# Picking one tile of source rows in 16 with TensorE instead of gathering it, in the message sums of a graph network

## The chip, the cores and the metric

The kernel runs as one program on one core of one Trainium2 chip. The metric is the device time of one execution in microseconds (us), lower is better. The same program is timed in several executions; the median is what counts.

## The reference, cut to what matters

A graph of 3125 nodes and 100,000 edges, sorted by target node, goes through four layers. The change lies in the fourth, of which this is the part that matters:

```python
src_f = x[src_idx]
dst_f = x[dst_idx]
msg_in = jnp.concatenate([src_f, dst_f, ew], axis=-1)
h = jax.nn.silu(msg_in @ mW1 + mb1)
messages = (h @ mW2 + mb2) * ew
aggregated = jax.ops.segment_sum(messages, dst_idx, num_segments=num_nodes)
```

The kernel multiplies each node by the source part and by the target part of `mW1` once, ahead of the edges. For each edge it then needs the 128 numbers of its source node (the gathered row), the 128 numbers of its target node, their sum through silu, times the edge weight, added up by target node. The product with `mW2` follows after the sums.

## The kernel before, in words

Edges are cut into 800 tiles of 125, four tiles are a quad (200 quads), and nodes into 25 windows of 125. Since edges are sorted by target, each quad touches one window, or two at a border: a step is one quad with one window, and there are 224 steps (`TEAMS`). Steps are grouped by four (`AHEAD`), which below is called a round: 56 rounds.

`message_sums` gives each engine its own loop. They meet only by semaphores; each engine works its own list strictly in the order written.

- GpSimd (POOL), `gather_quads`, line 553: for each quad four indirect DMAs, one per tile, each fetching 125 rows of `node_table` from HBM into a ring of 20 quads (`rows`). It waits for `kept`, which says that the ring's place is free.
- SyncE (SP), `pass_quads`: for each quad it frees the place of the quad four before, once DVE has used it (`added`), then waits for the quad's rows (line 572) and tells DVE with `here`. It also loads the indices (`now`).
- ScalarE (ACT), in step k: `copy_turned(k+1)` (line 1008), `widen(k+2)` (line 1003), the load of a one-hot tile (line 998), and silu in `apply(k)` (line 1013).
- TensorE (PE), in step k: `spread_rows(k)` (line 1051, target rows into `zp`), `turn_rows(k+2)` (line 1043, transposes the one-hot of target nodes), `sum_team(k-1)` (line 1060, sums messages by target node).
- VectorE (DVE), in step k: `weigh(k-1)` (lines 1092 and 1093), then z = `zp` + gathered rows (line 1110), `weigh_rows(k+2)` (line 1086), `add_team(k-2)` (line 1100).

Two waits matter for what follows. z of step k needs the gathered rows and `spread_rows(k)`. And `turn_rows(k+2)` needs `weigh_rows(k+2)`, which DVE issues only behind z of step k: so within a step PE's list goes on only after z.

Of the kernel before, what the change touches and what calls it, by code (L numbers as in the profile page):

```python
# [45 lines left out]
BIG = 1.0e30  # L46
ROUND = 12582912.0
EPS = 1e-5
GROUPS = (WIN + 3) // 4
CHUNK = 261  # L50
SIDE = 2 * CHUNK
# [357 lines left out]
def landed(i, dmas=1):  # L409

    return 16 * dmas * (i + 1)
# [121 lines left out]
def begin(eng, *sems):  # L533

    for sem in sems:
        eng.sem_inc(sem, AHEAD)
# [4 lines left out]
    return k - lag + 1 + AHEAD  # L541


def gather_quads(pool, table, rows, now, held_up, staged, kept, rows_in):
# [12 lines left out]
def pass_quads(sp, g, now, staged, rows_in, here, kept, step_done, held):  # L557

    def stage(n, group):
        sp.dma_start(now[:, n, :], g.tile_src[:, bass.ds(HALF * HALF * group, HALF * HALF)]).then_inc(staged[n], 16)  # L560

    def free(quad):
        last = sp.value_load(g.quad_done[0:1, bass.ds(quad, 1)], min_val=1 + AHEAD, max_val=TEAMS + AHEAD)
        sp.wait_ge(step_done, last)
        sp.sem_inc(kept, 1)

    def quads(i):
        for q in range(RING):
            if q >= held or not isinstance(i, int):
                free(RING * i + q - held)  # L570
            sp.wait_ge(rows_in[q], landed(i, HALF))
            sp.sem_inc(here, 1)  # L572
            if q % HALF == HALF - 1:
                stage(q // HALF, STAGES * i + STAGES + q // HALF)

    sp.sem_inc(kept, RING)
    for n in range(STAGES):
        stage(n, n)
    quads(0)
    with sp.Fori(1, QUADS // RING) as i:  # L580
        quads(i)
    for n in range(STAGES):
        sp.wait_ge(staged[n], landed(QUADS // RING))
# [372 lines left out]
                add_team(TEAMS - 2 + q, q + 2, ws[q])  # L956


def message_sums(nc, g, table, own):

# [3 lines left out]
    with Scope(nc) as sc:  # L964
# [8 lines left out]
        turn = sc.ps("turn", [P + 1, 2, 512])  # L973
        zp = sc.ps("zp", [P, 2, HALF, D])
        sums = sc.ps("sums", [P, 2, 512])
        kept, here = sc.sem("kept"), sc.sem("here")
        names = ("held_up", "acc_clear", "made", "weighed", "turned", "copied", "spread", "added", "active", "tailed", "weighted", "summed", "accd")
        held_up, acc_clear, made, weighed, turned, copied, spread, added, active, tailed, weighted, summed, accd = (sc.sem(x) for x in names)
# [4 lines left out]

        @block.gpsimd
        def _(pool):
            gather_quads(pool, table, rows, now, held_up, staged, kept, rows_in)

        @block.sync
        def _(sp):
            pass_quads(sp, g, now, staged, rows_in, here, kept, added, HALF)  # L990

        @block.scalar
        def _(act):
            begin(act, made, copied, active)

            def load_hot(k, q):
                act.wait_ge(made, after(k, AHEAD))
                act.dma_start(hot[:, q, :], g.hots[bass.ds(k, 1), :, :].rearrange("a p n -> (a p) n")).then_inc(hot_in[q], 16)

            def widen(k, m, q):  # L1000
                act.wait_ge(hot_in[q], landed(m))
                act.wait_ge(summed, after(k, AHEAD))
                act.copy(onehot[:, q, :, 0:P], hot[:, q, :].rearrange("p (j n) -> p j n", n=P)).then_inc(made, 1)

            def copy_turned(k, p):
                act.wait_ge(turned, after(k))
                act.wait_ge(spread, after(k, 2))
                act.activation(onehot_t[:, p, :], turn[:, p, 0:HALF * P], ACT.Identity).then_inc(copied, 1)

            def apply(k, p):  # L1010
                act.wait_ge(added, after(k))
                act.wait_ge(weighted, after(k, 2))
                act.activation(hidden[:, p, :, :], z[:, p, :, :], ACT.Silu).then_inc(active, 1)

            for q in range(AHEAD):
                load_hot(q, q)
            for q in range(2):
                widen(q, 0, q)
            copy_turned(0, 0)
            rounds = TEAMS // AHEAD  # L1020
            with act.Fori(0, rounds - 1) as i:
                for q in range(AHEAD):
                    k = AHEAD * i + q
                    copy_turned(k + 1, 1 - q % 2)
                    widen(k + 2, i + (q + 2) // AHEAD, (q + 2) % AHEAD)
                    load_hot(k + AHEAD, q)
                    apply(k, q % 2)
            for q in range(AHEAD):
                k = TEAMS - AHEAD + q
                copy_turned(k + 1, 1 - q % 2)  # L1030
                widen(k + 2, rounds - 1, (q + 2) % AHEAD)
                apply(k, q % 2)

        @block.tensor
        def _(pe):
            begin(pe, turned, spread, summed)

            def turn_rows(k, q):
                pe.wait_ge(made, after(k))
# [23 lines left out]
            def team(k, q):  # L1063
                spread_rows(k, q % 2)
                turn_rows(k + 2, (q + 2) % AHEAD)
                if not (isinstance(k, int) and k == 0):
                    sum_team(k - 1, (q - 1) % AHEAD)

            turn_rows(0, 0)
            turn_rows(1, 1)  # L1070
            for q in range(AHEAD):
                team(q, q)
            with pe.Fori(1, TEAMS // AHEAD) as i:
# [5 lines left out]
        def _(dve):  # L1079
            begin(dve, weighed, added, tailed, weighted, accd)  # L1080
            dve.memset(g.acc[:, :, :], 0.0).then_inc(acc_clear, 1)
            dve.wait_ge(acc_clear, 1)

            def weigh_rows(k, q):
                dve.wait_ge(summed, after(k, AHEAD))
# [26 lines left out]
                if not (first and k < 2):  # L1112
                    add_team(k - 2, p)

            def teams(i):
# [5 lines left out]
            weigh_rows(1, 1)  # L1121
            teams(0)
            with dve.Fori(1, TEAMS // AHEAD) as i:
                teams(i)
            weigh(TEAMS - 1, 1)
            add_team(TEAMS - 2, 0)
            add_team(TEAMS - 1, 1)
# [580 lines left out]
def prepare(nc, g, sc, src, dst, edge_weight, x, nodes):  # L1708
# [21 lines left out]
    g.step_quad, g.step_slot, g.quad_done = steps[32:33, 0:TEAMS + 1], steps[64:65, 0:TEAMS + 1], steps[96:97, 0:QUADS]  # L1730
    g.place = sc.sb("place", [1, 3 * (TEAMS + 1)], I32)
    g.pair = sc.sb("pair", [1, 2 * TEAMS], I32)
    g.tile_src = nc.dram_tensor("tile_src", (P, TILES + RING * HALF), I32, kind="Internal").ap()

    with Scope(nc) as s1:
# [32 lines left out]
        slot = s1.sb("slot_", [P, TEAMS])  # L1768
        over = s1.sb("over", [P, QUADS])
        slot_rows = s1.sb("slot_rows", [SIXTY, FIFTEEN, P], F16)  # L1770

        with Scope(nc) as s2:
            names = ("dst_in", "pre_in", "src_in", "ew_in", "pre_set", "zeroed", "drawn", "step", "bordered", "totalled", "compared", "summed")
            dst_in, pre_in, src_in, ew_in, pre_set, zeroed, drawn, step, bordered, totalled, compared, summed = (s2.sem(k) for k in names)
            names = ("sourced", "src_cut", "dst_parted", "src_parted", "ew_cut", "ew_left", "natural", "tiled", "picks", "picked", "kept", "x_in", "slotted", "rows_turned", "rows_kept", "tabled")
            sourced, src_cut, dst_parted, src_parted, ew_cut, ew_left, natural, tiled, picks, picked, kept, x_in, slotted, rows_turned, rows_kept, tabled = (s2.sem(k) for k in names)
# [8 lines left out]
            def _(sp):  # L1785
# [3 lines left out]
                sp.dma_start(src_i[:, :], src.rearrange("(r l) -> r l", l=rlen)).then_inc(src_in, 16)  # L1789
                sp.dma_start(ew_row[:, :], edge_weight.rearrange("(r l) -> r l", l=rlen)).then_inc(ew_in, 16)  # L1790
                wide(sp, x[:, :, :], by_window(nodes), x_in)
                sp.wait_ge(tiled, 1)
                sp.dma_start(g.tile_src, tile_src[:, :]).then_inc(kept, 16)
                sp.wait_ge(kept, 16)
                sp.wait_ge(x_in, 16 * len(PIECES))

            @block.gpsimd
# [29 lines left out]
            def _(dve):  # L1827
# [21 lines left out]
                dve.wait_ge(src_in, 16)  # L1849
                link(dve.tensor_copy(src_row[:, :], src_i[:, :]))  # L1850
                dve.sem_inc(sourced, 1)
                link(dve.tensor_copy(dst_parts[0][:, :], dst_row[:, :]))
                link(dve.tensor_tensor(dst_parts[1][:, :], dst_row[:, :], dst_parts[0][:, :], ALU.subtract))
                dve.sem_inc(dst_parted, 1)
# [528 lines left out]
def layer3(nc, g, a, x, table, out):  # L2383

    with Scope(nc) as sc:
# [22 lines left out]
        message_sums(nc, g, table, pb)  # L2408
# [150 lines left out]
```

## Time and profile before

| | us |
|---|---|
| median of 3 executions | 6612.52 (6611.82 to 6618.84) |
| the profiled execution | 6634.63 |
| its span, first to last instruction | 6632.9 |
| message sums within the span | about 5328 to 6571 |
| mean granted TensorE clock, whole span | 0.786 of full speed |

Over the span PE is busy 64%, DVE 52%, ACT 23%, POOL 60%. These shares are means over stages with different limits; the message sums are one stage, and rows of that stretch of time say what bounds it. A TensorE matmul in fp32 shows as two records here: a line of code that issues four matmuls leaves eight of them. A granted clock of 1.00 is 2.4 GHz, 0.50 is 1.2 GHz; values between are stretches in which it changed.

### The profile page before, as it was taken

The numbers are of one execution on the slowest core, as the hardware profiler recorded it, in microseconds if no ns is written. First come the engines' busy times: TensorE is split into PE (matmuls) and PEld (weight loads), VectorE is DVE, ScalarE is ACT, GpSimd is POOL, SyncE is SP. The second block draws the span as 40 slices with busy tenths as digits, with TensorE's granted clock in tenths as the row PEclk, the third lists the DMA queues.
The fourth block names the chain that finished last, engine by engine and source line by source line (L and its number), as shares of the span: only waits on it lengthen the run. The fifth ranks groups of instructions, "written<-read, shape, count | busy, mean of one in ns | idle before, by whom it ended". The sixth has DMA issues, their size and how long they took to land. (4 is left out here: it accounts for less than half of the span.)

```text
span 6632.9 us, 118789 instructions
## 1 busy us (share of the span) xinstructions
PE 4258.2 (64%) x28231; PEld 3627.6 (55%) x28232; DVE 3436.1 (52%) x8797; ACT 1545.7 (23%) x3206; POOL 3989.5 (60%) x3272
## 2 busy tenths in 40 slices
PE   7868774666666646666666466666664466666665
PEld 6755333555556535556665356665553355555554
DVE  8987225554545564545555645555556533333334
ACT  4764100111111111111111101111111134444443
POOL 0000003888888728878888288888881068888884
PEclk8999986788877777878777677777876777777777
DMA  5863441333333313333333133333331222222221
GB/s 158 216 166 112 119 119 47 87 91 86 90 87 92 91 47 84 87 88 92 92 91 89 46 79 92 92 89 90 89 89 33 52 67 65 66 65 65 66 65 46
DMA packets 599808, 578.37 MB, mean 87 GB/s; under 512 B 244747, under 2 KB 537024, under 8 KB 599702
## 3 DMA queue, kind: packets, MB, share of 16 engines
q0 software_dynamic: 260480, 241.33, 15.7%
q10 hardware_dynamic: 205535, 197.01, 10.2%
q1 hardware_dynamic: 133687, 138.75, 7.8%
q8 instruction: 51, 0.84, 0.1%
q14 instruction: 55, 0.45, 0.0%
HBM read 488.64 MB, written 84.64 MB: 86 GB/s over the span
## 5 line engine op out<-in xcount | busy, mean ns | idle before, releaser
L553 POOL DMA_INDIRECT rows<-row_table,now x2400 | 2967.7, 1237 | 1607.9 <-issue 1566.1
L553 POOL DMA_INDIRECT rows<-node_table,now x800 | 988.5, 1236 | 567.1 <-issue 567.1
L754 PE MATMUL zp<-rows,ident 125*125 x2700 | 975.4, 494 | 543.9 <-SPq L572 543.0
L840 DVE SCALAR_TENSOR_TENSOR z<-zp,own 125x512 f32<-125x512 f32 x672 | 464.8, 692 | 1374.8 <-PE zp L754 1347.9
L765 PEld LDWEIGHTS sums<-values,hot 125*125 125x125 f32 x5376 | 880.3, 225 | 165.5 <-issue 83.4
L751 PE MATMUL zp<-parts,hot_t 125*125 x8100 | 730.4, 249 | 372.0 <-DVE logit L847 264.6
L765 PE MATMUL sums<-values,hot 125*125 125x137 f32 x5376 | 906.9, 321 | 58.7 <-ACT hot L700 34.3
L754 PEld LDWEIGHTS zp<-rows,ident 125*125 125x125 f32 x2700 | 568.2, 234 | 657.9 <-issue 576.6
L751 PEld LDWEIGHTS zp<-parts,hot_t 125*125 125x125 bf16 x8100 | 691.8, 160 | 425.6 <-issue 420.6
L700 ACT CAST hot<-hot 125x500 f32<-125x500 bf16 x672 | 408.6, 608 | 2106.0 <-PE sums L765 1714.7
L851 DVE TENSOR_TENSOR values<-rows,xl 125x512 f32 (+1 forms) x672 | 461.6, 687 | 102.5 <-PE sums L765 80.5
L1043 PE MATMUL turn<-ident,onehot 125*126 125x125 f32 x904 | 179.2, 333 | 472.2 <-issue 451.8
L1110 DVE TENSOR_TENSOR z<-zp,rows 125x512 f32<-125x512 f32 x224 | 154.9, 691 | 630.0 <-SPq L572 495.1
L844 DVE TENSOR_REDUCE bent<-z 125x16 f32<-125x512 f32 x672 | 456.0, 679 | 1.6
L1043 PEld LDWEIGHTS turn<-ident,onehot 125*126 125x126 f32 x904 | 118.3, 169 | 517.7 <-issue 494.7
L1060 PE MATMUL sums<-values,onehot 125*125 125x129 f32 x1792 | 334.6, 349 | 0.0
L1051 PE MATMUL zp<-pb,onehot_t 126*125 x1792 | 332.3, 346 | 2.5
L1335 DVE TENSOR_SCALAR hot<-nodes,src_lo,src_unit 125x522 bf16<-125x522 f16 x896 | 315.1, 416 | 18.1 <-PE bank L1374 17.0
L1051 PEld LDWEIGHTS zp<-pb,onehot_t 126*125 126x125 f32 x1792 | 311.7, 260 | 10.2 <-issue 8.6
L1374 PE MATMUL bank<-hot,hot_dst 125*125 125x261 bf16 x1792 | 268.9, 296 | 67.8 <-DVE hot L1335 37.2
L1060 PEld LDWEIGHTS sums<-values,onehot 125*125 125x125 f32 x1792 | 310.0, 258 | 0.0
L1302 POOL DMA_DIRECT2D spread_slots<-slot_table x56 | 30.3, 541 | 397.7 <-DVE hot_t L1328 344.2
(447 smaller groups left out, 4918.8 us busy)
## 6 DMA issues: line engine op xcount, KB each, us to landing
hot<-hots ACTq DMA_DIRECT2D x896, 122.1 KB
hot_t<-hots_t ACTq DMA_DIRECT2D x678, 122.1 KB
rows<-row_table,now POOLq DMA_INDIRECT x2400, 3.5
counts<-pairs SPq DMA_DIRECT2D x55, 685.1 KB
spread_slots<-slot_table POOLq DMA_DIRECT2D x56, 488.3 KB
hots_t<-hot_t SPq DMA_DIRECT2D x112, 218.8 KB
hots<-hot_dst SPq DMA_DIRECT2D x112, 218.8 KB
pairs<-cells SPq DMA_DIRECT2D x25, 685.1 KB
```

The source lines that it names most:

```text
L553: pool.indirect_dma_start(rows[:, q, j, :], None, table, bass.IndirectOffsetOnAxis(ap=now[:, n, lane + j:lane + j + 1], axis=0)).then_inc( ...
L700: act.copy(hot32[:, q % 2, :], hot[:, q, :]).then_inc(made, 1)
L751: pe.matmul(zp[:, p, j, 0:ROW], hot_t[:, q, j * P:(j + 1) * P], own[part], start=part == 0 and j % 2 == 0, stop=False, skip_group_check=True)
L754: ins = pe.matmul(zp[:, p, 2 * half:2 * half + 2, 0:ROW], g.ident[0:P, 0:P], rows[:, bass.ds(at, 1), 2 * half:2 * half + 2, :].rearrange(" ...
L765: ins = pe.matmul(sums[:, p, 0:ACCW], hot32[:, p, j * P:(j + 1) * P], values[:, p, j, :], start=j == 0, stop=j == HALF - 1)
L840: dve.scalar_tensor_tensor(out=z[:, p, :, :], in0=zp[:, p, :, 0:D], scalar=0.0, in1=rows_of(own_att, HALF), op0=ALU.max, op1=ALU.mult).the ...
L844: dve.tensor_reduce(bent[:, p, :, :], z[:, p, :, :].rearrange("p j (h c) -> p j h c", h=HEADS), AX_X, ALU.add).then_inc(reduced, 1)
L851: dve.tensor_tensor(values[:, q % 2, :, 0:D].rearrange("p j (h c) -> p j h c", h=HEADS), rows[:, bass.ds(at, 1), :, 0:D].rearrange("p a j ...
L1043: ins = pe.transpose(turn[:, q % 2, j * P:(j + 1) * P], onehot[:, q, j, :], g.ident[0:P, 0:P])
L1051: ins = pe.matmul(zp[:, p, j, :], onehot_t[:, p, j * P:(j + 1) * P], own[:, bass.ds(w, 1), :].rearrange("p w f -> p (w f)"), start=True, s ...
L1060: ins = pe.matmul(sums[:, q % 2, 0:width], onehot[:, q, j, 0:P], values[:, q % 2, j, :], start=j == 0, stop=j == HALF - 1)
L1335: dve.tensor_scalar(hot[:, p % AHEAD, j, :], nodes[:, :], g.src_lo[:, s], g.src_unit[:, s], ALU.is_equal, ALU.mult).then_inc(hot_made, 1)
```

## The change

In every fourth quad (q % 4 == 3) the last tile is no longer gathered: 50 tiles of 800 (`PICKS`). Its rows are made on the chip. `pa`, the table's 25 windows of 125 nodes, is still in SBUF. ACT loads the tile's 125 source numbers (halved range, fp16) broadcast over the partitions and copies them into a PSUM bank (`lay`). DVE compares them with the node numbers of all 25 windows, in three cuts of 9, 8 and 8 windows (`point`), which gives one-hots in `at`, free at this time. PE multiplies the 25 one-hots by the 25 windows of `pa` and adds up in the bank `mix` (`pick`, 25 fp32 matmuls in the same three cuts). ACT copies the result to SBUF and stores it to HBM (`store_picked`), and SP loads it into the ring (`fetch`), two quads ahead of its use.

Picks 0 and 1 are made before the first step, pick i+2 in round i, for 48 of the 56 rounds; the last 8 rounds have none. The source numbers are written to HBM in `prepare` (one more DVE instruction on 100x125 and two small DMAs).

```diff
+def by_engine(q, picks):
+    return picks and q % PICK == PICK - 1
...
-            for j in range(HALF):
+            for j in range(HALF - 1 if by_engine(q, picks) else HALF):
                 pool.indirect_dma_start(rows[:, q, j, :], None, table,
...
+            if fetch is not None and q % PICK == PICK - 3:
+                fetch(i, q + 2)
+            if by_engine(q, fetch is not None):
+                hold(sp, rows_in[q], landed(i, HALF - 1), fetching)
+                sp.wait_ge(fetched[q // PICK], landed(i, len(PIECES)))
...
+            def lay(t):
+                act.wait_ge(src_in, landed(t))
+                act.copy(wide_src[:, 0:P], src[:, :]).then_inc(laid, 1)
+                act.wait_ge(laid, t + 1)
+
+            def store_picked(t):
+                act.wait_ge(mixed, len(CUTS) * (t + 2))
+                if not (isinstance(t, int) and t == 0):
+                    act.wait_ge(stored, landed(t - 1, len(PIECES)))
+                act.copy(picked[:, :], mix[:, 0:D]).then_inc(evicted, 1)
+                act.wait_ge(evicted, t + 1)
+                wide(act, store[bass.ds(t, 1), :, :].rearrange("a p f -> (a p) f"), picked[:, :], stored)
...
+            with act.Fori(0, PICKS - 2) as i:
+                four_steps(i)
+                store_picked(i + 2)
+                lay(i + 3)
+                load_src(i + 4)
+            with act.Fori(PICKS - 2, rounds - 1) as i:
+                four_steps(i)
...
+            def pick(t, r):
+                pe.wait_ge(noded, len(CUTS) * t + r + 1)
+                if r == 0 and not (isinstance(t, int) and t == 0):
+                    pe.wait_ge(evicted, t)
+                for w in range(*CUTS[r]):
+                    ins = pe.matmul(mix[:, 0:D], hot_n[:, w, :], pa[:, w, :], start=w == 0, stop=w == WIN - 1)
+                ins.then_inc(mixed, 1)
...
+            def team(k, q, t=None):
                 spread_rows(k, q % 2)
                 turn_rows(k + 2, (q + 2) % AHEAD)
+                if t is not None and q:
+                    pick(t, q - 1)
...
+            def point(t, r):
+                lo, hi = CUTS[r]
+                if r == 0:
+                    dve.wait_ge(laid, t + 1)
+                dve.wait_ge(mixed, len(CUTS) * t + r + 1)
+                dve.tensor_tensor(hot_n[:, lo:hi, :], rows_of(wide_src[:, 0:P], hi - lo), each(nodes[:, lo:hi], P), ALU.is_equal).then_inc(noded, 1)
...
+            def teams(i, picking=True):
                 quads, slots = step_quads(nc, dve, g, AHEAD * i)
                 for q in range(AHEAD):
+                    if picking and q < len(CUTS):
+                        point(i + 2, q)
                     team(i, q, quads[q], slots[q])
```

On TensorE, one step (the second of a round) in the loop over rounds, before:

```order
L436 ISA
L436 TENSOR_LOAD steps
L436 ISA x2
L1048 REGISTER_ALU
L1051 ISA
L1051 MATMUL zp<-pb,onehot_t 125x128 x4
L1039 REGISTER_ALU
L1043 MATMUL turn<-ident,onehot 126x125 x4
L1060 MATMUL sums<-values,onehot 125x129 x4
```

The same step in the changed kernel:

```order
L441 ISA
L441 TENSOR_LOAD steps
L441 ISA x2
L1124 REGISTER_ALU
L1127 ISA
L1127 MATMUL zp<-pb,onehot_t 125x128 x4
L1115 REGISTER_ALU
L1119 MATMUL turn<-ident,onehot 126x125 x4
L1107 ISA
L1111 MATMUL mix<-pa,at 125x128 x9
L1136 MATMUL sums<-values,onehot 125x129 x4
```

Nine matmuls now stand between the transposes and the sums (eight in the third and in the fourth step, none in the first).

On ScalarE, the end of a round in the first loop of the changed kernel, behind the last silu (before, that silu was followed by the loop's branch):

```order
L1044 ACTIVATE hidden<-z 125x512
L1057 ISA
L1059 REGISTER_ALU
L1060 COPY picked<-mix 125x128
L1061 REGISTER_ALU
L143 ISA
L143 DMA picked_nodes<-picked 112x128
L143 ISA
L143 DMA picked_nodes<-picked 13x128
L1052 REGISTER_ALU
L1053 CAST wide_src<-src 125x125
L1049 ISA
```

The copy of the picked rows, two stores and the copy of the next tile's sources into PSUM now stand between two rounds on this engine.

## Rows read from the trace of the kernel before

**Rows 1.** Groups of instructions, 5328 to 6575: shapes, count | busy, mean ns | idle before.
```profile
L553 POOL DMA_INDIRECT rows<-node_table,now x800 | 988.5, 1236 | 567.1 <-issue 567.1
...
L1110 DVE TENSOR_TENSOR z<-zp,rows 125x512 f32<-125x512 f32 x224 | 154.9, 691 | 630.0 <-SPq L572 495.1 <-PE zp L1051 134.2 <-issue 0.2
...
L1100 DVE TENSOR_TENSOR acc<-acc,sums 125x129 f32 x224 | 65.0, 290 | 77.1 <-issue 73.6 <-PE sums L1060 3.0
```

**Rows 2.** Waits, 5328 to 6575: who waited <- for whom: total us, times, longest.
```profile
DVE z L1110 <- SPq L572: 495.1, 142, 6.9
...
DVE z L1110 <- PE zp L1051: 134.2, 75, 3.4
```

**Rows 3.** Timeline, start of the stage: start, us, engine, line.
```profile
5330.92 1.21 POOL L553 DMA_INDIRECT rows<-node_table,now  x1 [323.52 <-issue]
5331.42 0.61 ACT L1003 CAST onehot<-hot 125x500 f32<-125x500 bf16 x1 [23.28 <-DMA hot<-hots]
...
5334.23 2.05 PE L1051 MATMUL zp<-pb,onehot_t 126*125 x8
...
5339.29 0.69 DVE L1110 TENSOR_TENSOR z<-zp,rows 125x512 f32<-125x512 f32 x1 [6.95 <-SPq L572]
```

**Rows 4.** Timeline, end of the stage.
```profile
6561.76 1.21 POOL L553 DMA_INDIRECT rows<-node_table,now  x1 [0.30 <-issue]
...
6565.52 0.69 DVE L1110 TENSOR_TENSOR z<-zp,rows 125x512 f32<-125x512 f32 x1 [3.86 <-SPq L572]
```

**Rows 5.** Timeline, steps that catch up at the full clock, 5930 to 5938.
```profile
5930.36 0.69 DVE L1110 TENSOR_TENSOR z<-zp,rows 125x512 f32<-125x512 f32 x1 [2.47 <-PE zp L1051]
...
5931.23 0.62 PE L1043 MATMUL turn<-ident,onehot 125*126 125x125 f32 x4 [1.02 <-issue]
...
5931.68 1.05 PE L1060 MATMUL sums<-values,onehot 125*125 125x129 f32 x8
...
5934.20 0.69 DVE L1110 TENSOR_TENSOR z<-zp,rows 125x512 f32<-125x512 f32 x1 [0.22 <-PE zp L1051]
...
5937.76 0.69 DVE L1110 TENSOR_TENSOR z<-zp,rows 125x512 f32<-125x512 f32 x1 [0.52 <-PE zp L1051]
```

**Rows 6.** Timeline of DVE, a third and fourth step of a round at the full clock.
```profile
6378.01 0.69 DVE L1110 TENSOR_TENSOR z<-zp,rows 125x512 f32<-125x512 f32 x1 [1.19 <-PE zp L1051]
...
6381.40 0.69 DVE L1110 TENSOR_TENSOR z<-zp,rows 125x512 f32<-125x512 f32 x1 [1.04 <-PE zp L1051]
```

**Rows 7.** Timeline, a step that catches up at the low clock, 5907 to 5913.
```profile
5907.17 0.69 DVE L1110 TENSOR_TENSOR z<-zp,rows 125x512 f32<-125x512 f32 x1 [4.45 <-SPq L572]
...
5908.89 1.93 PE L1060 MATMUL sums<-values,onehot 125*125 125x129 f32 x8
...
5910.62 1.91 PE L1051 MATMUL zp<-pb,onehot_t 126*125 x8
...
5912.76 0.69 DVE L1110 TENSOR_TENSOR z<-zp,rows 125x512 f32<-125x512 f32 x1 [1.91 <-PE zp L1051]
```

**Rows 8.** PE groups before the stage, 5300 to 5328, at the full clock.
```profile
L2485 PE MATMUL bank<-m,at 128*125 128x128 f32 x100 | 11.2, 273 | 1.1 <-PEq L105 1.1
```

**Rows 9.** Windows: length, busy of PE, PEld, DVE, ACT, POOL; granted clock, DMA share, GB/s.
```profile
5904.00:5906.50 2.50, 0.00 (x0) 0.00 (x0) 0.00 (x0) 0.00 (x0) 1.94 (x2) 1.00 0.36 82
5907.00:5912.50 5.50, 4.46 (x20) 4.22 (x20) 1.83 (x5) 3.90 (x5) 4.30 (x4) 0.50 0.18 38
5931.00:5941.00 10.00, 7.55 (x60) 6.80 (x60) 4.85 (x15) 7.75 (x11) 8.17 (x7) 1.00 0.30 75
...
5350.00:6550.00 1200.00, 744.30 (x4375) 693.11 (x4374) 411.08 (x1095) 529.60 (x764) 962.51 (x780) 0.76 0.27 65
```

**Rows 10.** Groups of ACT over the whole span, a copy of 125 columns out of PSUM.
```profile
L257 ACT ACTIVATE ft<-bank,cols 128x125 f32<-128x125 f32 x3 | 1.1, 359 | 0.0
```

**Rows 11.** Line 138, stores issued by SP in two pieces: ns min/median/max.
```profile
L138 SPq DMA_DIRECT2D hots<-hot_dst x224: 317/317/1033, 69.5 to 453.7; - x112
```

More of the change, by code:

```diff
@@ L48 @@
 EPS = 1e-5
+PICK = 4
+PICKS = QUADS // PICK
+CUTS = ((0, 9), (9, 17), (17, WIN))
+LAST = (PICKS - 2) // GROUP
+assert RING % PICK == 0 and PICK == HALF and E // RROWS == 2 * HALF * P and (PICKS - 2) % GROUP == 0 and LAST < BLOCKS - 1
 GROUPS = (WIN + 3) // 4
@@ L541, in after, with gather_quads @@
     return k - lag + 1 + AHEAD
-def gather_quads(pool, table, rows, now, held_up, staged, kept, rows_in):
+def by_engine(q, picks):
+    return picks and q % PICK == PICK - 1
+def gather_quads(pool, table, rows, now, held_up, staged, kept, rows_in, picks=False):
     with pool.Fori(0, QUADS // RING) as i:
@@ L956, in _, with message_sums @@
                 add_team(TEAMS - 2 + q, q + 2, ws[q])
-def message_sums(nc, g, table, own):
+def message_sums(nc, g, table, pa, at, own):
     width = D + 1
@@ L975, in message_sums @@
         sums = sc.ps("sums", [P, 2, 512])
+        wide_src = sc.ps("wide_src", [P, 512])
+        mix = sc.ps("mix", [P, 512])
+        picked = sc.sb("picked", [P, D])
+        nodes = sc.sb("nodes", [P, WIN])
+        src = sc.sb("src", [P, P], F16)
+        hot_n = at[0:P, :].rearrange("p (w e) -> p w e", e=P)
+        store = g.picked_nodes
+        names = ("src_in", "laid", "numbered", "noded", "mixed", "evicted", "stored", "fetching")
+        src_in, laid, numbered, noded, mixed, evicted, stored, fetching = (sc.sem(x) for x in names)
+        fetched = [sc.sem(f"fetched{n}") for n in range(RING // PICK)]
         kept, here = sc.sem("kept"), sc.sem("here")
@@ L985, in _, with fetch @@
         def _(pool):
-            gather_quads(pool, table, rows, now, held_up, staged, kept, rows_in)
+            gather_quads(pool, table, rows, now, held_up, staged, kept, rows_in, picks=True)
         @block.sync
         def _(sp):
-            pass_quads(sp, g, now, staged, rows_in, here, kept, added, HALF)
+            def fetch(i, q):
+                t = RING // PICK * i + q // PICK
+                hold(sp, stored, landed(t, len(PIECES)), fetching)
+                wide(sp, rows[:, q, HALF - 1, :], store[bass.ds(t, 1), :, :].rearrange("a p f -> (a p) f"), fetched[q // PICK])
+            pass_quads(sp, g, now, staged, rows_in, here, kept, added, HALF, fetch, fetched, fetching)
         @block.scalar
@@ L1020, in _, with four_steps @@
             rounds = TEAMS // AHEAD
-            with act.Fori(0, rounds - 1) as i:
+            def four_steps(i):
                 for q in range(AHEAD):
@@ L1032, in _ @@
                 apply(k, q % 2)
+            act.wait_ge(src_in, landed(PICKS + 1))
+            act.wait_ge(stored, landed(PICKS - 1, len(PIECES)))
         @block.tensor
@@ L1061, in sum_team @@
                 ins.then_inc(summed, 1)
-            def team(k, q):
+            def team(k, q, t=None):
                 spread_rows(k, q % 2)
                 turn_rows(k + 2, (q + 2) % AHEAD)
+                if t is not None and q:
+                    pick(t, q - 1)
                 if not (isinstance(k, int) and k == 0):
                     sum_team(k - 1, (q - 1) % AHEAD)
+            for t in range(2):
+                for r in range(len(CUTS)):
+                    pick(t, r)
             turn_rows(0, 0)
@@ L1071, in _ @@
             for q in range(AHEAD):
-                team(q, q)
-            with pe.Fori(1, TEAMS // AHEAD) as i:
+                team(q, q, 2)
+            with pe.Fori(1, PICKS - 2) as i:
+                for q in range(AHEAD):
+                    team(AHEAD * i + q, q, i + 2)
+            with pe.Fori(PICKS - 2, TEAMS // AHEAD) as i:
                 for q in range(AHEAD):
@@ L1121, in _ @@
             weigh_rows(1, 1)
+            for t in range(2):
+                for r in range(len(CUTS)):
+                    point(t, r)
             teams(0)
-            with dve.Fori(1, TEAMS // AHEAD) as i:
+            with dve.Fori(1, PICKS - 2) as i:
                 teams(i)
+            with dve.Fori(PICKS - 2, TEAMS // AHEAD) as i:
+                teams(i, False)
             weigh(TEAMS - 1, 1)
@@ L2407, in layer3 @@
         layer3_rows(nc, g, at, m1, u1, m2, mb1, ub1, mb2, pa, pb, own, joint, each_edge, table)
-        message_sums(nc, g, table, pb)
+        message_sums(nc, g, table, pa, at, pb)
         with Scope(nc) as s1:
```

35 lines of the change are left out of this document (29 added, 6 removed).

## The prediction

> **What bounds the kernel now.** I read the groups of the stage first, then its waits, then the timeline at its start, its end and in its middle, and last the granted clock in short windows. The groups show POOL issuing 800 gathers with a mean of 1.24 us and 0.3 us between them, without waiting for another engine [rows 1]. The first starts at 5330.92 and the last at 6561.76 [rows 3, 4], so one takes 1230.84 / 799 = 1.54 us, and a quad 6.16 us. The waits say the same: DVE's z waits 495 us for SP, which passes on the landed rows, and 134 us in 75 steps for PE [rows 2]. The stage is bound by the issue of gathers. The 75 steps are where compute catches up: a border gives a quad two steps, and the second finds its rows there. These steps show what compute can do alone. At the full clock z follows z after 3.84 us in the first step of a round (5930.36 to 5934.20), 3.56 in the second [rows 5] and 3.39 later on [rows 6]: 14.2 us a round. At the low clock a step takes 5.59 us [rows 7]. POOL needs 200/224 of four quads for a round, 22.0 us. So compute has 7.8 us to spare per round at the full clock, and nothing (22.1 us) at the low one.
>
> **What is removed.** 50 gathers at 1.54 us are 77 us of POOL. If nothing else became late, the last z would come at 6565.5 - 77.0 = 6488.5, and all that follows (5.5 us to the end of the stage, then the rest) would move with it.
>
> **What is added in a round, engine by engine.**
> PE: 25 fp32 matmuls, 50 records. 100 records of the same width and type took 11.2 us at the full clock [rows 8], 0.112 each: 5.6 us, 2.0 for the cut of nine, 1.8 for each of eight. At the low clock eight records start 1.73 us apart [rows 7], 0.216 each: 10.8 us. They do not fill PE's idle time. PE sits idle after the spread until z has been made, since the transposes wait for an instruction behind z; the picks stand behind those transposes and ahead of the sums and of the next spread. In a step bound by compute all of it lies on the path z, transposes, pick, sums, spread, z. While rows are late it is hidden in the idle time; when rows are there it is added in full.
>
> DVE: from 129 columns in 290 ns and 512 in 691 ns [rows 1] a column costs 1.05 ns, and cuts of 1125 and 1000 columns 1.33 and 1.20 us, 3.7 us a round. The cut delays the weighing behind it by about 1 us, but PE asks for that only after the next transposes: covered, except in the first step of a round.
>
> ACT: two copies of 128 and 125 columns. The nearest row has 125 columns in 0.36 us, with a bias that these lack [rows 10]; I take 0.3 each, with 0.2 and 0.4 as bounds. Two stores at 0.32 us issue each [rows 11] and one load come to it.
>
> **The end of a round** is the new wait. From z of the fourth step: transposes start at +0.87 and the next PE line 0.45 later [rows 5]; the pick's last cut ends at +3.1, its result is there at +3.3; ACT, which has nothing else left in the round, copies it (+3.6), waits for that copy, issues two stores (+4.3), and copies the next sources (+4.65). Only then may DVE compare (1.33 us, +6.0), and behind that comparison stand in DVE's list the weighing (0.7, tail 0.15) and z of the next round's first step: +6.9. Without this detour the step would take 3.84 + 1.8 = 5.64. The detour costs 1.25 us a round. Its bounds: 0, if the steps are hidden by late rows, and 2.5, if each of its six hand-overs costs 0.2 more than I count. It also leaves PE idle from the spread's end (+5.0) to the next transposes (+7.8), 2.8 us, because ACT's next two table loads and its copies start late.
>
> So a round with a pick takes, when compute bounds, 14.2 + 5.6 + 1.25 = 21.05 us at the full clock. POOL's part of it is now 20.6 us. The gather and the compute are almost level.
>
> **The clock** decides. In the stretch 5931 to 5941 three steps with short gaps went through 60 records at 1.00; from 5904 to 5906.5 PE had nothing, and the next step ran at 0.50 [rows 9]. The new round has 130 records in 21 us, as dense as that good stretch, so most of it should run at the full clock. But its one gap of 2.8 us is about as long as that idle stretch, which was part of a longer gap. A low step costs 2.1 us more without a pick (5.5 against 3.4) and 16 x 0.104 = 1.7 on top of that with one: 3.0 on average. Bounds: no low step per round (21.05) to one each (24.05); all low would be 34 us, which the good stretch excludes. I take 0.45 low steps a round, 1.35 us: 22.4 us, since the gap is shorter than that one and breaks only one step in four.
>
> TensorE's transposes might not help to hold the clock: in the good stretch they are 12 of 60 records [rows 9], too few to tell. The Trainium skill (TensorE: Matmul & The Clock Gate, Part 4, PE-mode transpose) says that transposes do not count as busy; by that rule the gap would reach to the end of the transposes, 3.3 us, and one low step a round, the slower rival below, would be likely. No run here shows it yet.
>
> **The start.** The picks 0 and 1 stand before the first step. The sources land about when the first hot tile does (5331.4) [rows 3]; then copy, compare 1.3, 50 records, most at the low clock (9 us), copy and stores and copy 1.3, compare 1.3, 50 records 5.6, again 1.3, and what now runs from 5331.42 to the end of the first spread (5336.3, 4.9 us [rows 3]; 4.1 at the full clock). First z at about 5357 instead of 5339.3. POOL is not held by this: its ring takes 20 quads.
>
> **The sum.** z of step 192 comes 48 rounds later, the last z 31 steps after that; these steps have no pick and POOL is far ahead, so 7 x 14.2 + 3.56 + 2 x 3.4 = 109.8 us. Last z = 5357 + 109.8 + 48 R. With R = 22.4: 6542.0, 23.5 us earlier than 6565.5. The profiled execution of 6634.6 us would become 6611, and the median of the runs, 6612.5, becomes 6589. The same line gives the points that decide: at R = 21.3 and below POOL bounds again (6488.5), at R = 22.9 the change gives nothing, and each 0.1 us of a round is 4.8 us.
>
> At nothing I count: the preparation (one DVE instruction on 125 columns, two small DMAs; 0 to 2 us), and SP's fetches. A pick is stored at step 4t-5, while SP asks for it only after freeing quad 4t-3, two steps or 7 us later. If that cover failed, SP would wait at line 572's place and `here` would come late for a whole quad.
>
> **Rivals.**
> (a) POOL stays the bound: the clock holds and the detour hides behind late rows. For it: 21.05 is below 21.3. Against it: any low step in a round ends it. 77 us less: 6536. The Trainium skill (same page, Back-to-back issue gap) gives about 81 ns per load and matmul pair of 128 columns; by it 50 records are 4.05 us and not 5.6, a round 19.5, and this rival would win. The fp32 rows say 112 ns, and I hold to them.
> (b) Slower: the gap at the round's end lets the clock fall in every round. One mechanism, at the hand-over PE, ACT, DVE, PE. It decides from R = 22.9, that is 0.6 low steps a round, or a detour dearer by 1.8 us in all. With one low step: R = 24.05, last z 6621, 56 us more: 6668. For it: the gap's length and the granted mean of 0.76 over the stage before, where such gaps are frequent [rows 9]. Against it: the density of the rest.
> (c) No change: R between 22.6 and 23.2, within 13 us, which is 0.2% and about what a measurement of this kernel can tell from none.
> (d) The change does not do what it says, the picked rows arriving late so that POOL's saving is lost in SP: excluded by the order above unless a store takes over 7 us.
>
> **Chances.** Forecast (R 21.6 to 22.6, 6552 to 6599) 0.35; (a) 0.12; (c) 0.20; (b) 0.33, of which a third lies beyond 6665. (d) is within (b). Faster 0.47, same 0.20, slower 0.33. The likeliest case's own range is 6552 to 6599; the range for 8 in 10 reaches from (a), 6535, to 6665.
>
> **What would show it.** Right: 750 gathers at 1.54 us, but now POOL waits for `kept` in the second half; z waits mostly for PE; z to z of a full round in rounds 10 to 47 at 21 to 23 us; the step into a new round 6.5 to 7.5 us, with DVE's first cut waiting for ACT's copy; the granted clock of the stage above 0.85; the last rounds at about 14 us. Wrong: z still waiting for SP throughout (a), a step into a round over 8 us or a granted clock under 0.85 in the picked rounds (b), a pick whose 50 records cost other than 5.6 us at the full clock, or a first z far from 5357.

## The result, and the profile after

| | before | changed |
|---|---|---|
| median of 4 executions, us | 6615.7 | 6663.3 |
| lowest to highest | 6611.8 to 6621.6 | 6655.5 to 6674.4 |
| the profiled execution (span) | 6634.6 (6632.9) | 6665.1 (6663.3) |

The change made the kernel slower: ratio 1.0070, interval 1.0058 to 1.0083, 48 us. The forecast was 23 us faster; 6663 lies inside the range, whose upper end was 6665. What happened is rival (b). One of the four executions of e7 below took 6950 us at a lower granted clock, and the times and ratios given leave it out.

The stage begins 13 us earlier in the changed kernel's profiled execution, for reasons that lie before it. So times are counted from the first gather. Timeline of the changed kernel: the first gather, the first z, z of step 192 (the first step without a pick in its round), the last gather and the last z.

```profile
5317.94 1.21 POOL L563 DMA_INDIRECT rows<-node_table,now  x1 [321.23 <-issue]
...
5345.90 0.69 DVE L1205 TENSOR_TENSOR z<-zp,rows 125x512 f32<-125x512 f32 x1 [3.39 <-PE zp L1127]
...
6486.61 0.69 DVE L1205 TENSOR_TENSOR z<-zp,rows 125x512 f32<-125x512 f32 x1 [1.44 <-PE zp L1127]
...
6540.66 1.21 POOL L563 DMA_INDIRECT rows<-node_table,now  x1 [0.31 <-issue]
...
6597.17 0.69 DVE L1205 TENSOR_TENSOR z<-zp,rows 125x512 f32<-125x512 f32 x1 [1.17 <-PE zp L1127]
```

From first gather to last z it is 1279.2 us; before it was 1234.6 [rows 3, 4]. That is 44.6 us more, practically the whole difference of 47.7 us between the medians. A round with picks took (6486.61 - 5345.90) / 48 = 23.76 us, where 22.9 was the point at which the change gives nothing. The last gather ends 56 us before the last z, so POOL no longer sets the end.

The waits of the changed kernel, 5328 to 6640 (who waited <- for whom: total us, times, longest), answer to rows 2:

```profile
DVE z L1205 <- PE zp L1127: 349.3, 170, 4.3
...
DVE at L1177 <- ACT wide_src L1053: 201.2, 49, 7.4
...
PE turn L1119 <- ACT onehot L1034: 162.2, 52, 3.3
ACT picked L1060 <- PE mix L1111: 123.3, 50, 9.6
POOL rows L563 <- SPq L575: 78.3, 38, 6.4
```

z's 495 us for SP are gone altogether, so the picked rows arrive in time and rival (d) is out; z waits for PE now. POOL itself waits 78 us for a free place in the ring, and its last gather starts 1222.7 us after its first, only 8 us sooner than before (1230.8): of the 77 us that it saved it gives back about 69. And there are two waits with about one entry a round each that were absent or small before: DVE's compare for ACT's copy of the sources, and PE's transposes for ACT's widening (14.8 us in 13 entries before).

Both stand in one place, the end of a round. Timeline of the changed kernel from z of a fourth step (start, us, engine, line):

```profile
5842.46 0.69 DVE L1205 TENSOR_TENSOR z<-zp,rows 125x512 f32<-125x512 f32 x1 [2.86 <-PE zp L1127]
...
5843.79 1.91 PE L1111 MATMUL mix<-pa,at 125*125 125x128 f32 x16
5845.54 1.05 PE L1136 MATMUL sums<-values,onehot 125*125 125x129 f32 x8
...
5845.81 0.27 ACT L1060 COPY picked<-mix 125x128 f32<-125x128 f32 x1 [1.99 <-PE mix L1111]
...
5846.24 0.85 ACTq L143 DMA_DIRECT2D picked_nodes<-picked  x2
...
5846.42 1.04 PE L1127 MATMUL zp<-pb,onehot_t 126*125 x8
...
5847.19 0.27 ACT L1053 CAST wide_src<-src 125x125 f32<-125x125 f16 x1 [1.11 <-issue]
...
5847.60 1.33 DVE L1177 TENSOR_TENSOR at<-wide_src,nodes 125x1125 f32<-125x1125 f32 x1 [3.79 <-ACT wide_src L1053]
...
5849.52 0.68 DVE L1205 TENSOR_TENSOR z<-zp,rows 125x512 f32<-125x512 f32 x1
...
5850.74 0.65 PE L1119 MATMUL turn<-ident,onehot 125*126 125x125 f32 x4 [3.28 <-ACT onehot L1034]
...
5854.37 0.69 DVE L1205 TENSOR_TENSOR z<-zp,rows 125x512 f32<-125x512 f32 x1 [0.75 <-PE zp L1127]
```

The chain reads as the prediction wrote it: last cut, copy, two stores, sources, compare, and only then z of the next round, 7.06 us after the last one. The cut of eight takes 1.75 us (5843.79 to 5845.54), 0.11 a record, as the prediction priced it. PE's spread ends at 5847.46 and nothing runs on PE until 5850.74. What that gap does shows in the granted clock. Windows of the changed kernel (length, busy of PE, PEld, DVE, ACT, POOL, then granted clock, DMA share, GB/s), the last of them over most of the stage:

```profile
5848.00:5850.00 2.00, 0.00 (x0) 0.00 (x0) 2.00 (x4) 1.68 (x2) 1.70 (x2) 1.00 0.31 59
5850.00:5852.00 2.00, 1.26 (x11) 1.26 (x12) 1.58 (x4) 1.97 (x3) 1.70 (x2) 0.98 0.36 95
5852.00:5854.00 2.00, 2.00 (x11) 1.92 (x9) 0.77 (x2) 1.60 (x3) 1.39 (x3) 0.50 0.27 57
5854.00:5858.00 4.00, 2.98 (x15) 2.79 (x14) 2.85 (x6) 1.22 (x2) 3.39 (x3) 0.50 0.28 72
...
5360.00:6440.00 1080.00, 775.51 (x5919) 739.43 (x5918) 504.82 (x1041) 457.27 (x726) 815.74 (x661) 0.90 0.28 68
```

PE had nothing to do at 1.00, and then works at 0.50, 1.2 GHz, for the rest of one step and part of the next. This happens in 41 of the 43 rounds from 4 to 46, behind a gap that is 3.28 us long nearly every time. The last two steps of a round all ran at 1.00. Over the stage the clock was 0.90. That is far better than the 0.76 of before [rows 9], but before a low step could be hidden behind late rows, and now z never waits for rows, so that a low step is on the path.

Of the prediction's signs, z's wait for PE, the compare's wait for ACT, the step into a round (7.23 us in the mean) and a clock above 0.85 came as for the forecast; the round, 23.76, missed its 21 to 23. Neither sign named for (b), a step over 8 us or a clock under 0.85, came, and yet (b) is what happened: the signs did not tell the two apart, the round did.

### The profile page after: what moved, and what is told of

Same layout as the page of the kernel before. It is cut to its first block and busy times, and to the rows that moved or that the text cites. A ratio compares the mean times of both kernels' runs of the same rounds, so it can differ in the third digit from the quotient of the medians.

```text
span 6663.3 us, 125447 instructions
## 1 busy us (share of the span) xinstructions
PE 4401.6 (66%) x30731; PEld 3776.8 (57%) x30732; DVE 3612.4 (54%) x8950; ACT 1548.5 (23%) x3293; POOL 3924.8 (59%) x3222
## 5 line engine op out<-in xcount | busy, mean ns | idle before, releaser
L563 POOL DMA_INDIRECT rows<-node_table,now x750 | 927.5, 1237 | 617.7 <-issue 537.2
L1119 PE MATMUL turn<-ident,onehot 125*126 125x125 f32 x904 | 151.6, 294 | 356.9 <-issue 194.7
L1111 PE MATMUL mix<-pa,at 125*125 125x128 f32 x2500 | 332.2, 292 | 10.2 <-DVE at L1177 10.2
L1111 PEld LDWEIGHTS mix<-pa,at 125*125 125x125 f32 x2500 | 321.4, 208 | 10.6 <-DVE at L1177 10.6
L1119 PEld LDWEIGHTS turn<-ident,onehot 125*126 125x126 f32 x904 | 100.3, 148 | 399.4 <-issue 227.4
L1177 DVE TENSOR_TENSOR at<-wide_src,nodes 125x1125 f32<-125x1125 f32 x150 | 185.6, 1239 | 201.2 <-ACT wide_src L1053 201.2
L1127 PE MATMUL zp<-pb,onehot_t 126*125 x1792 | 277.1, 305 | 0.9 <-ACT onehot_t L1039 0.3
L875 DVE TENSOR_TENSOR acc<-acc,sums 125x137 f32 x672 | 194.0, 289 | 147.1 <-PE sums L781 107.9
```

The costliest lines, as they stand in the source:

```text
L563: pool.indirect_dma_start(rows[:, q, j, :], None, table, bass.IndirectOffsetOnAxis(ap=now[:, n, lane + j:lane + j + 1], axis=0)).then_inc( ...
L1111: ins = pe.matmul(mix[:, 0:D], hot_n[:, w, :], pa[:, w, :], start=w == 0, stop=w == WIN - 1)
L1127: ins = pe.matmul(zp[:, p, j, :], onehot_t[:, p, j * P:(j + 1) * P], own[:, bass.ds(w, 1), :].rearrange("p w f -> p (w f)"), start=True, s ...
```

## The experiments

Two theories were set against each other. A: the hand-over at the round's end (PE, ACT, DVE, PE) holds up the next round and opens the gap in which the clock falls. B: what costs is the picks' own 50 records, in series behind z. The filler of e4, e8 and e10 writes columns of `mix` that nothing reads. All ratios are to the kernel before on the same chip. "Round" is the mean over the 48 rounds with picks, from the timeline as above; steps are means over rounds 4 to 46, named by their place in the round. Two things follow from the prediction's line (last z = first z + 48 rounds + tail): a round under 21.3 leaves the gathers as the bound, one over 22.9 is a loss.

| kernel | median us | ratio (interval) | round us | clock 5360 to 6440 |
|---|---|---|---|---|
| changed | 6663.3 | 1.0070 (1.0058 to 1.0083) | 23.76 | 0.90 |
| e1 sources laid early | 6617.9 | 0.9996 (0.9986 to 1.0006) | 22.78 | 0.90 |
| e2 and stores late | 6551.4 | 0.9897 (0.9880 to 0.9914) | 20.26 | 0.97 |
| e3 picks ahead of transposes | 6546.2 | 0.9889 (0.9872 to 0.9905) | 20.14 | 0.88 |
| e4 filler matmuls in the gap | 6568.1 | 0.9920 (0.9904 to 0.9937) | 21.58 | 1.00 |
| e5 e2 and e3 | 6546.4 | 0.9887 (0.9871 to 0.9904) | 20.03 | 0.90 |
| e6 4 matmuls a pick | 6545.1 | 0.9885 (0.9868 to 0.9901) | 20.37 | 0.85 |
| e7 all tiles gathered too | 6674.8 | 1.0083 (1.0063 to 1.0103) | 23.90 | 0.89 |
| e8 e1 and filler | 6548.9 | 0.9898 (0.9881 to 0.9914) | 20.98 | 1.00 |
| e9 table loads out of the loop | 6638.4 | 1.0027 (1.0013 to 1.0041) | 23.04 | 0.91 |
| e10 filler transposes | 6561.7 | 0.9906 (0.9890 to 0.9923) | 21.59 | 1.00 |

**e4, the clock alone.** The edit, in PE's list behind the spread of a round's first step:

```diff
+                if t is not None and q == 0:
+                    pe.wait_ge(evicted, t)
+                    for w in range(12):
+                        pe.matmul(mix[:, 256:256 + D], g.ident[0:P, 0:P], pa[:, w, :], start=True, stop=True)
```

> 12 fp32 matmuls with no use (24 records, 2.7 us at the full clock) are put into the gap at the start of each round with picks, behind the spread of its first step. Nothing else changes. Theory A with the clock as the dear half: the granted clock of the picked rounds rises from 0.90 to over 0.97, steps of 4.84 and 5.3 us become 4.0, those of 7.1 become 5.4, a round 21.8 to 22.2 us: 6575 to 6600 us, although PE does more work. If the clock's fall does not come from the gap or costs little, 6663 us or, where the added matmuls lie on the path, up to 130 us more.

PE and DVE of e4 at the end of a round, timeline:

```profile
5873.02 1.04 PE L1127 MATMUL zp<-pb,onehot_t 126*125 x8
...
5873.90 2.79 PE L1144 MATMUL mix<-pa,ident 125*125 125x128 f32 x24
...
5876.11 0.69 DVE L1209 TENSOR_TENSOR z<-zp,rows 125x512 f32<-125x512 f32 x1
...
5877.34 0.65 PE L1119 MATMUL turn<-ident,onehot 125*126 125x125 f32 x4 [0.66 <-ACT onehot L1034]
...
5880.12 0.68 DVE L1209 TENSOR_TENSOR z<-zp,rows 125x512 f32<-125x512 f32 x1
```

The useless matmuls fill the gap down to 0.66 us, nothing waits longer for them, and the kernel gets 95 us faster than the changed one (medians of two chips, on which the kernel before took 6615.7 and about 6620 us; by the ratios it is 1.5%). The clock is 1.00 throughout. The step into a round keeps its 7.05 us (7.23 in the changed kernel), so the hand-over is all there; the other three go from 5.05, 6.17 and 5.27 to 4.00, 5.36 and 5.16. This splits the round of 23.76 in two: 21.58 that the order of work costs at the full clock, and 2.18 that the clock costs. The changed kernel's own trace agrees: its two rounds without a fall took 21.80 and 21.83 us. The time is 7 us below the expected range.

**e1 and e2, the hand-over in two parts.** e1 lays the next sources at the start of the fourth step, once DVE has made its last cut; e2 also moves the copy and the stores of the picked rows behind the first silu of the next round.

```diff
+                    if early and q == AHEAD - 1:
+                        act.wait_ge(noded, len(CUTS) * (i + 3))
+                        lay(i + 3)
+                        load_src(i + 4)
                     copy_turned(k + 1, 1 - q % 2)
...
                     apply(k, q % 2)
+                    if late and q == 0:
+                        store_picked(i + 1)
```

> The copy of the next sources into PSUM (and their load) is taken from the end of the round to the start of its fourth step; the stores stay at the end. Theory A (the hand-over PE, ACT, DVE, PE at the round's end holds up the first z of a round and opens a gap in PE in which the clock falls): DVE's wait of 201 us for ACT's copy goes, the step into a new round falls from 7.2 to about 5.4 us, PE's gap from 3.3 to about 2.2 us, a round from 23.75 to 21 to 22 us: 6550 to 6585 us. Theory B (the picks' own matmuls, in series behind z, are the cause and the hand-over is harmless): within 10 us of the changed kernel, 6655 to 6675 us.

e1 gave neither theory's number. The wait of DVE for the sources is gone, and the step into a round fell from 7.23 to 5.44 us as theory A has it. But the next two steps went up, from 5.05 and 6.17 to 5.55 and 6.62. PE of e1 at the end of a round, with z of the next round's first step:

```profile
5919.43 1.04 PE L1131 MATMUL zp<-pb,onehot_t 126*125 x8
...
5920.70 0.69 DVE L1209 TENSOR_TENSOR z<-zp,rows 125x512 f32<-125x512 f32 x1 [0.25 <-PE zp L1131]
...
5922.92 0.65 PE L1123 MATMUL turn<-ident,onehot 125*126 125x125 f32 x4 [2.46 <-ACT onehot L1034]
...
5923.40 1.05 PE L1140 MATMUL sums<-values,onehot 125*125 125x129 f32 x8
...
5924.33 2.01 PE L1131 MATMUL zp<-pb,onehot_t 126*125 x8
```

A gap of 2.46 us is left, and behind it a spread of 2.01 us at the low clock: ACT still waits for the last cut before it comes to the widening that PE needs. Theory A had the gap, but took it to shrink enough. It lacked a second thing: z comes earlier now, but ACT's widening does not, so the transposes start 2.22 us behind z (5920.70 to 5922.92), where it was 1.22 (5849.52 to 5850.74).

> As e1, and the copy and the stores of the picked rows also leave the round's end: they come behind the silu of the next round's first step. Theory A: nothing of the hand-over is left, ACT reaches its table loads and copies in time, PE's gap shrinks to about 1 us, a round takes 14.2 + 6 = 20 to 20.5 us at a granted clock near 1, below the 20.6 us of POOL: gathers bound again, 77 us less than before, 6535 to 6550 us. Theory B: 6655 to 6675 us.

e2 takes most of that wait away too (39 us are left for PE's transposes, from 162). Its waits, 5330 to 6560:

```profile
DVE z L1210 <- PE zp L1132: 274.9, 159, 3.8
...
POOL rows L563 <- issue: 226.5, 743, 0.3
DVE z L1210 <- SPq L588: 89.1, 36, 4.3
```

z waits for gathered rows again in 36 steps, and POOL waits for the ring 0.9 us in all. 6551 us, 68 less than before on that chip: 1.4 us above the upper end of theory A's range, and 100 us below B's. The picks' records are all there, in the same place, so the hand-over alone was enough.

**e8, what e1 lacked.** e1 with the filler of e4.

> e1 with the 24 records of e4 in the gap. e1 took away DVE's wait but gained only 46 us, since the gap before the transposes (2.5 us) stayed and the clock still fell (granted 0.90). Theory A: with the clock held, steps of 5.55 and 6.62 us become 4.3 and 5.4, a round 20.3 to 20.9 us: 6540 to 6560 us. If e1's lost time was not the clock's, 6605 to 6630 us.

6549 us, round 20.98, clock 1.00. The clock is worth 1.8 us a round between e1 and e8, for the same order of work plus 24 records. But the first step came out at 5.02 us and not 4.3, against 4.00 in e4: this is the widening that comes late, at the full clock. Between e4 and e8 the step into a round loses 1.70 us and the first step gains 1.02, so at the full clock laying the sources early is worth 0.60 us a round, and not the 1.8 by which its own step got shorter.

**e3, the picks in PE's idle time.**

```diff
                 spread_rows(k, q % 2)
+                if t is not None and q:
+                    pick(t, q - 1)
                 turn_rows(k + 2, (q + 2) % AHEAD)
-                if t is not None and q:
-                    pick(t, q - 1)
```

> The picks stand ahead of the transposes in PE's list, where PE idles about 1 us for z in each step. Theory B (series behind z is what costs): 0.9 us less in each of three steps, and less idle time for the clock: a round of 20.5 to 21.3 us, 6540 to 6555 us. Theory A: the hand-over and its gap stay (ACT gets the picked rows 0.9 us sooner), the clock still falls in most rounds: a round of 21.3 to 22.3 us, 6550 to 6600 us. If the idle time is not really usable, 6663 us.

6546 us, theory B's number. This edit moves the picks into the time in which PE waits for z anyway: here in a step of e3 the pick follows the spread and the transposes follow the pick without idle time. (The rows here are late.)

```profile
5900.01 1.91 PE L1111 MATMUL mix<-pa,at 125*125 125x128 f32 x16
5901.94 0.62 PE L1119 MATMUL turn<-ident,onehot 125*126 125x125 f32 x4
5902.40 1.05 PE L1136 MATMUL sums<-values,onehot 125*125 125x129 f32 x8
5903.53 1.13 PE L1127 MATMUL zp<-pb,onehot_t 126*125 x8
5908.39 0.62 PE L1119 MATMUL turn<-ident,onehot 125*126 125x125 f32 x4 [3.72 <-issue]
```

It is not B alone, though. The order of the hand-over stays, but it starts sooner, because the last cut is done sooner. ACT's copy of the picked rows in e3, 1.72 us behind z of the fourth step, where it was 3.35 (5842.46 to 5845.81):

```profile
5881.36 0.69 DVE L1205 TENSOR_TENSOR z<-zp,rows 125x512 f32<-125x512 f32 x1 [1.11 <-PE zp L1127]
...
5883.08 0.27 ACT L1060 COPY picked<-mix 125x128 f32<-125x128 f32 x1 [0.36 <-PE mix L1111]
```

So A and B do not exclude each other. Each names a term of the same sum. Taking A's away suffices (e2); taking B's away suffices too, with the part of the hand-over that goes with it, for no run here shortens the picks and leaves the hand-over's time alone. The round only had to lose 2.5 us to come below 21.3. The clock still falls in e3 (0.88 over the stage), as behind the 3.72 us of the first block's last row; the end is bound by the gathers all the same (z waits 181 us for SP, in 72 steps), so it costs little or nothing.

**e6, few matmuls.** One matmul for each of the first two cuts, two for the last; 21 of the 25 are left out, so the picked rows are not the right ones.

```diff
-                for w in range(*CUTS[r]):
+                for w in (range(*CUTS[r])[0], range(*CUTS[r])[-1]) if r == 2 else (CUTS[r][0],):
```

> Of the 25 matmuls of a pick 4 are left (one per cut, two in the last); the picked rows are therefore not the right ones. Compare, copies, stores and the order stay. PE's work on the path falls by 21 x 0.224 = 4.7 us a round at the full clock. Theory A says that the hand-over (about 1.8 us) and the gap remain, but with the matmuls gone even rounds with low steps (17 to 20.5 us) are shorter than POOL's 20.6: 6540 to 6555 us. If it stays above 6590, neither the matmuls nor their place is what matters, but the copies and compares.

6545 us. The compare, the copies, the stores and the hand-over with its wait (133 us of DVE's compare for ACT, from 201) are all in this kernel, and cost nothing as long as PE's round is short. As in e3 the hand-over starts sooner, about 2.0 us behind z.

**e7, is the saving worth anything?** `picks=True` and the fetches are taken out of the calls of `gather_quads` and `pass_quads`.

> All 800 tiles are gathered again and used; the picks are made and stored as in the changed kernel, but not fetched. POOL needs 22.0 us a round instead of 20.6. Theory A: rounds of 23.76 us are bound by compute, so the 50 gathers are worth nothing: 6655 to 6672 us, the same as the changed kernel. If the changed kernel's time still hung on POOL, it would be up to 77 us more: 6700 to 6740 us.

Its round takes 23.90 us, as in the changed kernel, though POOL gathers 50 tiles more; z waits 352 us for PE, and POOL's last gather still starts 52 us before the last z. The median lies 3 us above what was expected, and the interval of its ratio overlaps that of the changed kernel. The 50 gathers saved were worth nothing, or at most some us, once compute was the bound.

**e5, both orders.**

> The edits of e2 and e3 together: sources laid early, stores late, picks ahead of the transposes. Theory A: compute has slack in every round (18 to 19 us at the full clock against 20.6 of POOL), gathers bound from start to end, the whole 77 us of the 50 gathers: 6538 to 6545 us, no more than 5 us below e3. If something other than POOL's issue still costs, it stays at e3's 6546.

6546.4 us: no better than e3, and 1.4 us above the range expected by theory A. From first gather to last z it is 1152.2 us (e3: 1155.0), 82 less than before. A gather takes 1.53 us there from first to last, and POOL waits 1.8 us for the ring: the gathers are the bound, and more slack in compute buys nothing.

**e9, the table loads.** One silu on a column ahead of the loop makes the two table loads of each round unnecessary.

```diff
             copy_turned(0, 0)
+            act.activation(primed[:, :], g.eps[0:P, :], ACT.Silu)
```

> The changed kernel with one small silu ahead of the loop; with it the two table loads at the start of each round (2 x 1.28 us) leave the loop, nothing else changes. The transposes of a round's first step wait for the widening, which stands behind the first of these loads. Theory A: the gap of 3.3 us falls to about 2.0 and the clock falls less often; the step after it from 5.05 to 4.0 or 4.5 us; a round from 23.76 to 21.5 to 22.8 us: 6560 to 6620 us. If the loads lie beside other work, 6655 to 6670 us.

Between the two expectations: 6638 us, a round of 23.04, 0.7 less. In the profile of e9 PE still idles 2.92 us at the round's end and the clock still falls (0.91); the range of theory A assumed a gap of 2.0. It doesn't fall always, and a round of e9 that ran at 1.00 from end to end shows what the loads cost at the full clock (z of the first step, the transposes, z of the second step, z of the next round's first; then the window):

```profile
5925.81 0.69 DVE L1207 TENSOR_TENSOR z<-zp,rows 125x512 f32<-125x512 f32 x1
...
5926.68 0.62 PE L1121 MATMUL turn<-ident,onehot 125*126 125x125 f32 x4 [2.92 <-ACT onehot L1035]
...
5929.39 0.69 DVE L1207 TENSOR_TENSOR z<-zp,rows 125x512 f32<-125x512 f32 x1 [0.79 <-PE zp L1129]
...
5947.36 0.68 DVE L1207 TENSOR_TENSOR z<-zp,rows 125x512 f32<-125x512 f32 x1
...
5925.80:5947.30 21.50, 15.17 (x130) 14.41 (x130) 10.71 (x25) 7.73 (x14) 17.29 (x14) 1.00 0.30 73
```

The round is 21.55, against 21.58 in e4. In the 11 such rounds the first step takes 3.57 us, against 4.00 in e4, but the step into a round 7.43, against 7.05: at the full clock the loads cost next to nothing in sum. So what e9 gained came from the clock: it fell in 32 of 43 rounds, in the changed kernel in 41.

**How often the clock fell, by the gap ahead of a round's first transposes.** Counted in rounds 4 to 46; the gap is the same within 0.1 us in all of a kernel's rounds, in e2 in most of them.

| kernel | gap, us | rounds with a fall behind it |
|---|---|---|
| changed | 3.28 | 41 of 43 |
| e9 | 2.92 | 32 |
| e1 | 2.46 | 29 |
| e2 | 1.11 | 4 |
| e4, e10 | 0.66 | 0 |

A gap of one and the same length is followed by a fall in one round and by none in another, so its length alone doesn't settle it.

**e10, do transposes hold the clock?**

```diff
+                    for w in range(24):
+                        pe.transpose(mix[:, 256:256 + P], pa[:, w, 0:P], g.ident[0:P, 0:P])
```

> As e4, but the 24 records in the gap are transposes and not matmuls, of about the same duration. If transposes hold the clock like matmuls: the same as e4, a round 21.6 us, granted clock 1.00, 6565 to 6575 us. The Trainium skill (TensorE: Matmul & The Clock Gate, Part 4, PE-mode transpose) says that transposes do not count as busy: by it the clock falls as in the changed kernel, granted 0.90, and the time is 6655 to 6680 us. Theory A says nothing on this; from the rows of before (transposes are 4 of 20 records of a step) I hold the first for somewhat likelier.

The gap filled with transposes, PE of e10:

```profile
5874.86 2.78 PE L1144 MATMUL mix<-ident,pa 125*125 125x125 f32 x24
5878.30 0.65 PE L1119 MATMUL turn<-ident,onehot 125*126 125x125 f32 x4 [0.66 <-ACT onehot L1034]
```

Clock 1.00, round 21.59, 6562 us: the same as e4. fp32 transposes held the clock here as matmuls did. (A transpose leaves one record and an fp32 matmul two, so these are 24 transposes, against 12 matmuls in e4.) The sentence of the Trainium skill on transposes (TensorE: Matmul & The Clock Gate, Part 4, PE-mode transpose), by which the clock doesn't rise for them, is not borne out here: with transposes alone in the gap it stayed at 1.00, and the measurement decides. Whether transposes alone would bring a low clock up no run shows.

## Why the prediction was wrong

What it got right: POOL was the bound, a gather costs 1.54 us, compute would bind in rounds with picks, the hand-over's chain step by step, and the two numbers that decide (21.3 and 22.9). The experiments bear the two numbers out: every kernel with a round under 21.3 ended 68 to 75 us below before, every one over 22.9 ended above it, and e1, with 22.78, on it.

By terms of its sum, with what the profile shows:

| term | predicted | measured | effect on the end |
|---|---|---|---|
| first z after the first gather, later than before by | 17.7 | 19.6 | +1.9 |
| round at the full clock, x 48 | 21.05 | 21.58 (e4) | +25 |
| low clock in a round, x 48 | 1.35 | 2.18 (changed less e4) | +40 |
| last z after z of step 192 | 109.8 | 110.6 | +0.8 |

These add up to 68 us, which is the distance between the forecast of -23.5 and the measured +44.6.

The step that failed is the share of low steps: "I take 0.45 low steps a round, 1.35 us ... since the gap is shorter than that one and breaks only one step in four". The clock fell in 41 of 43 rounds, 0.95 a round, and not 0.45. In part the gap was longer, 3.28 us and not 2.8; but e9 with 2.92 and e1 with 2.46 still had a fall in 0.74 and 0.67 of their rounds. How often a gap of that length is followed by a fall was not known from rows, and was guessed to the good side.

The price of a fall was wrong the other way. The prediction took 3.0 us (and its own 2.1 without a pick and 3.8 with one make 3.4, since three steps in four have a pick). Measured is 2.18 a round, 2.3 a fall: the first step, without a pick, took 5.11 us in place of 4.00, and the second 7.08 in place of 5.37 in about half the rounds. Rival (b)'s round, 24.05, is near the measured 23.76 partly by luck: its price was 0.7 too high for each fall and its full-clock round 0.53 too low. With the low clock's 2.18 in place of 1.35 and nothing else changed, the round is 21.05 + 2.18 = 23.23 and the kernel 16 us slower: the forecast's sign hung on this term.

The second term mis-sized is the full-clock round, by 0.53 us. In e4 the first step takes 4.00 instead of 3.56 and the step into the round 7.05 instead of 6.9; the two stores occupy ACT's queue for 0.85 us instead of 0.64. Without the table loads the first step takes 3.57 at the full clock, but the step into the round 7.43 (e9), so what makes the round as a whole 0.53 longer stays open. The mis-size of this term alone, with the predicted 1.35, would have made the round 22.93, just on the point of no change.

Of the rivals, (b) named the mechanism, its place and its threshold, and got 0.33 against 0.35 for the forecast. With compute at 21.05 and the gathers at 20.6 us a round, the honest reading was that the sign hung on a term of which the profile gave no row. (a) was excluded by the same term, and its price of 77 us is what e2, e3, e5, e6 and e8 came near to.

## What to carry to other kernels

When work is taken off the bounding engine and put on others, compare the new round of each engine's chain with the new round of the bound, not busy shares: here PE had 38% of its time free (744.3 of 1200 us busy, [rows 9]), but a round with the picks took 21.58 us at the full clock, where the gathers needed 20.6. Put added work where its engine already waits (e3), and move hand-overs between engines off the loop's turn (e2); either made the same change worth 1.0 to 1.1% instead of costing 0.7%. If an idle gap of TensorE lies on the path and can't be closed, try to fill it: here work of no use in the gap gave 95 us back (e4).

## What the hardware showed that I had not expected

- 24 filler records of 0.116 us in a gap of about 3 us raised the granted clock from 0.90 to 1.00 and shortened the kernel by 95 us, while PE did more work.
- fp32 transposes hold the clock like fp32 matmuls (e10: 1.00, 6562 us; e4: 1.00, 6568 us).
- How often the clock falls behind a gap changes gradually with its length: 29 of 43 rounds at 2.46 us (e1), 32 at 2.92 (e9), 41 at 3.28 (changed), none at 0.66 (e4).
- A fall cost 2.3 us (2.18 a round, in 41 of 43 rounds): the first step grew from 4.00 to 5.11 us, and the second from 5.37 to 7.08 in about half the rounds.
- A store issued in pieces of 112 and 13 partitions occupies ACT's queue for 0.85 us in all, against 0.32 for each of two such issues on SP [rows 11].
